# Cross-attention SSM and mixture of experts on one core: projections and scatters spread over the scan's steps, with three products of a zero tile in four steps of eight

## The chip, the cores and the metric

The kernel runs on one core of a Trainium2 chip. The metric is the device time of one execution in microseconds (us), as the median of several runs. One further execution was taken by the profiler; its stages and single instructions are what the rest of this text reads.

## What is computed

```
x = x + xattn(ctx, layernorm(x), ...)          # a selective state-space layer (SSM)
    u     = silu(conv4(in_proj ctx) + conv_b)
    B, C, dt_lo = x_proj u
    delta = softplus(dt_proj dt_lo + dt_b);  A = -exp(A_log)
    state = state * exp(delta*A) + (delta*u) * B     # over 256 positions, 256 channels x 16 states
    y     = (sum_n state*C + D*u) * silu(z)
x = x + moe(layernorm(x), Wg, w1, w2)
    probs = softmax(x Wg); the best 2 of 8 experts for each token, 320 places an expert
    out   = sum over the 2 of gate * w2(relu(w1(row)))
```

Four batches of 256 tokens, 256 columns, hidden size 1024 in each of the 8 experts, all float32. The reference adds dt_b inside the softplus, and drops a token from an expert that is full.

## The kernel before, in words

The order of every engine's work is written out by hand, with semaphores between them; SyncE (SP), GpSimd (POOL), ScalarE (ACT), TensorE (PE) and VectorE (DVE) each have one program.

**The start (to about 20 us).** PE forms the input projection of batch 0 and the product of dt_proj with x_proj (L823); DVE runs the 4-tap convolution (L1089, L1092), ACT the SiLU; then `dt_bias` (L701, a product with one row) and `dt_part` (L707) make delta's argument; ACT takes Abs, Exp and Ln of it (`decay_exps`, `logs`), and DVE puts the softplus together. `keep_clock` (L692) is a product of ones that nothing reads.

**The scan (32 steps; about 20 to 162 us).** Step g = 8*b + p treats two of the 16 states of batch b. POOL's `drive` (L342) makes delta*u*B; ACT's `decay` (L529, four instructions) writes exp(delta*A) into one of two slots in PSUM; DVE runs the recurrence (L1131, two scans) one step ahead and multiplies by C (`mult`, L1142), which PE has spread over the partitions (`c_cast`, L749); PE adds the products into y by eight transposes (`add_state`, L766). `c_cast(g+1)` waits for `mult(g)`, since it writes the bank that this one reads.

Between the steps each engine has the pieces that prepare the next batch and finish the last one:
- for the next batch: PE `project` (L695, B and C), `dt_bias`, `dt_part`; ACT `b_rows`, `hi_rows` (L493, L487), `decay_exps`, `logs`; DVE `lo_rows` (L1070), `softplus_t`; POOL `softplus_d`, `softplus_w`, `softplus_delta`, `delta_u` (L349 to L364); PE `conv` (L715) for the batch behind it, and ACT `silu_pieces` (L599), which also needs `z_rstd` of POOL (L306 to L314).
- for the last batch: DVE `gate_y` (L1151), POOL `add_x`, DVE `row_stats` and `variance`, POOL `row_rstd`; PE `turn_x1` (L776), ACT `x1_turned` (L539), PE `logits` (L792), DVE `choose` (L1176 to L1183, the two best experts), PE `counts` (L802 to L811), DVE `place` (L1207 to L1219, the row of each token in its expert and its weight), ACT `row_scales`, `top_exp`, `normalise`, and POOL `send` (L387): four scatters of a batch's rows to the list of expert rows in memory.

**The turn to the experts (162 to 175 us).** The last batch's `gate_y` to `place` stand one behind the other. SP loads expert 0's rows (`rows_in(0)`, L257) when the scatters of batches 0 to 2 have landed; PE's `place_rows` (L915) turns them, and the products of L1026 add the rows of the last batch without a trip through memory. POOL meanwhile splits w1 (L417), and sends the last batch's rows.

**The experts (175 us to the end).** PE runs 48 + 48 products of 320 columns an expert (L935 to L937), with the weights of the next expert prepared beside them. In expert 0 `turn_rows(1)` stands after half of the second product.

Of the kernel before, what the change touches and what calls it, by code (L numbers as in the profile page):

```python
# [48 lines left out]
NCH = ALOG + DS  # L49
# [22 lines left out]
V0BANK = DABANK + 3  # L72
# [9 lines left out]
def cols(b):  # L82
    return slice(b * L, (b + 1) * L)

# [5 lines left out]
def build(nc, x, ctx_t, inproj_t, xproj_t, dt_small, conv_w, chan, wg, w1, w2, consts, slot_numbers, sel,  # L90
# [4 lines left out]
    with ExitStack() as ctx:  # L95
# [100 lines left out]
        def decays(r):  # L196
# [6 lines left out]
            "sp_abs sp_exp sp_ln sp_d sp_t sp_w delta_done du_done a_exp a_neg "  # L203
# [93 lines left out]
        def _(pool):  # L297
# [82 lines left out]
            def send(b):  # L380

                pool.wait_ge(s["gates_done"], b + 1)
                pool.wait_ge(s["slots_done"], b + 1)
                for j in range(b * BT, (b + 1) * BT):
                    pool.wait_ge(s["xn_done"], j + 1)
                    for k in range(TOPK):
                        nc.gpsimd.indirect_dma_start(  # L387
                            xe_dram, bass.IndirectOffsetOnAxis(ap=sloti[:, j, k:k + 1], axis=0),
                            xrow[:, j, k, :], None, bounds_check=SLOTS - 1, oob_is_err=False
                        ).then_inc(s["scattered1" if b == B - 1 else "scattered0"], 16)  # L390

            for j in range(1, STEPS):
                b, p = divmod(j - DRING, PAIRS)
                if b >= 0 and b + 1 < B:
# [8 lines left out]
                if b >= 1:  # L403
                    if p == 0:
                        add_x(b - 1)
                    if p == (1 if b == B - 1 else 2):
                        row_rstd(b - 1)
                    if p == 7:
                        if b == 1:
                            pool.wait_ge(s["xe_filled"], 16)  # L410
                        send(b - 1)
                drive(j)
            send(B - 2)
            for m in range(WP):
# [6 lines left out]
            send(B - 1)  # L421
# [44 lines left out]
        def _(act):  # L466
# [28 lines left out]
            def decay_exps(b, bank):  # L495
# [3 lines left out]
                nc.scalar.activation(spe, by_chunk(bank), ACT.Abs).then_inc(s["sp_abs"], 1)  # L499
                act.wait_ge(s["sp_abs"], b + 1)  # L500
# [84 lines left out]
            nc.scalar.activation(anegs[:], ch[:, :, ALOG:ALOG + DS], ACT.Exp).then_inc(s["a_exp"], 1)  # L585
            decay_exps(0, V0BANK)
            logs(0)
            act.wait_ge(s["sel_in"], 16)
            nc.scalar.activation(sels[:], brow[0:XPC, 0:BC], ACT.Copy).then_inc(s["sel_done"], 1)
# [15 lines left out]
            for g in range(STEPS):  # L605
# [10 lines left out]
                if nb < B:  # L616
                    if p == (1 if b else 2):
                        b_rows(nb)
                        hi_rows(nb)
                        decay_exps(nb, WBANK)  # L620
                        logs(nb)
                if b >= 1:
                    if p == (2 if b == B - 1 else 4):
                        x1_turned(b - 1)
                    if p == (3 if b == B - 1 else 5):
                        row_scales(b - 1)
                        top_exp(b - 1)
                        for j in range((b - 1) * BT, b * BT):
                            normalise(j)
                if b == B - 1 and p == 5:  # L630
                    for m in range(WP):
                        split_w1(0, m)
                if p == (7 if b < B - 2 else 6):
# [51 lines left out]
        def _(pe):  # L685

            pe.wait_ge(s["ones_made"], 1)

# [16 lines left out]
            def dt_part(b, k, bank):  # L705
                for c in range(EC):
                    ins = nc.tensor.matmul(by_chunk(bank)[:, c, :], wdt[:, k, c * P:(c + 1) * P],  # L707
                                           u[:, k, cols(b)], start=False, stop=(k == EC - 1),
                                           skip_group_check=True)
                return ins  # L710
# [60 lines left out]

            def turn(rows, first, last):
# [45 lines left out]
            for c, bank in ((0, WBANK), (1, CBANK)):  # L818
                nc.tensor.matmul(ps[:, bank, 0:L], inps[:, c * P:(c + 1) * P], ctxs[:, cols(0)],
                                 start=True, stop=True).then_inc(s["xe0_psum"], 1)  # L820
            pe.wait_ge(s["dts_in"], 16)
# [4 lines left out]
            dt_bias(V0BANK)  # L826
# [572 lines left out]
```

## Time and profile before

| | |
|---|---|
| median of 3 runs | 313.26 us (311.56 to 313.32) |
| the profiled execution | 314.71 us |
| its span, first to last instruction | 312.6 us |
| granted TensorE clock, mean | 0.866 |
| busy PE, DVE, ACT, POOL | 264.2, 218.2, 170.0, 218.7 us |
| scan, from DVE's first to its last | 19.7 to about 160 us |
| first product of the experts | 175.22 us |

Start times are from the span's first instruction. In a timeline row the first number is the start, the second the time from there to the end of the merged instructions, then the engine, line, operation, output<-inputs and their number.
### The profile page before, as it was taken

What the parts mean: (1) busy time and instruction counts of PE and PEld (TensorE: products, weight loads), DVE (VectorE), ACT (ScalarE), POOL (GpSimd) and SP (SyncE); (2) the same over time, 40 slices, a digit from 0 to 9 for tenths busy, and PEclk for the clock granted to TensorE, in tenths of its full rate; (3) what the DMA queues carried; (4) which work ended last, traced back from release to release, by engine and by line L of the source; (5) the groups of instructions that cost most, each with busy time, mean ns of one, the idle gap of its engine ahead of it and who ended that gap; (6) DMA issues with size and microseconds to landing.
All of it is one profiled execution on the core that took longest, in us unless ns stands there. A gap on an engine that the chain in (4) does not pass through costs nothing. (4 is left out here: it accounts for less than half of the span.)

```text
span 312.6 us, 4937 instructions
## 1 busy us (share of the span) xinstructions
PE 264.2 (85%) x1520; PEld 232.9 (75%) x1520; DVE 218.2 (70%) x383; ACT 170.0 (54%) x367; POOL 218.7 (70%) x182
## 2 busy tenths in 40 slices
PE   8969877886957947697699899999999999999960
PEld 7748665755746636576488799999999999999950
DVE  2489999987699788998945346857575757566610
ACT  1678579463893457638404347646473737373410
POOL 1839699959939699698371686677777777777652
PEclk9995989596796976756559999999999999999995
DMA  6459540052001442110055144454555454644011
GB/s 171 172 142 338 167 170 0 3 191 113 0 17 54 163 155 122 51 53 0 34 199 181 64 103 163 176 210 167 209 167 208 166 207 165 208 166 167 33 40 38
DMA packets 14929, 40.24 MB, mean 129 GB/s; under 512 B 2906, under 2 KB 9756, under 8 KB 11968
## 3 DMA queue, kind: packets, MB, share of 16 engines
q1 hardware_dynamic: 11648, 33.02, 31.2%
q0 software_dynamic: 2816, 6.32, 5.8%
q10 hardware_dynamic: 448, 0.70, 0.9%
q8 instruction: 8, 0.13, 0.2%
q14 instruction: 9, 0.07, 0.1%
HBM read 32.58 MB, written 8.49 MB: 131 GB/s over the span
## 5 line engine op out<-in xcount | busy, mean ns | idle before, releaser
L342 POOL TENSOR_TENSOR dbu<-du,bsb 128x1024 f32<-128x1024 f32 x31 | 72.5, 2359 | 6.2 <-ACT bsb L515 3.6
L1131 DVE TENSOR_TENSOR_SCAN h<-ps,dbu 128x512 f32<-128x512 f32 x64 | 74.5, 1206 | 1.1 <-ACT ps L529 0.7
L529 ACT ACTIVATE ps<-delta,anegs 128x255 f32<-128x255 f32 x128 | 53.0, 462 | 7.5 <-DVE h L1131 7.3
L1296 DVE SCALAR_TENSOR_TENSOR htlo<-ps,hthi 128x320 fp32r<-128x320 f32 x64 | 30.5, 487 | 35.2 <-ACT hthi L655 35.2
L766 PE MATMUL ps<-cst,hc 128*128 128x128 f32 x256 | 48.4, 351 | 0.0
L749 PE MATMUL ps<-stack,sels 64*128 64x256 f32 x64 | 19.5, 393 | 33.1 <-DVE hc L1142 29.6
L426 POOL TENSOR_TENSOR w2lo<-w2raw,w2hi 128x512 fp32r<-128x512 f32 x30 | 38.4, 1303 | 9.8 <-ACT w2hi L646 9.6
L766 PEld LDWEIGHTS ps<-cst,hc 128*128 128x128 f32 x256 | 39.4, 182 | 4.6 <-issue 2.2
L749 PEld LDWEIGHTS ps<-stack,sels 64*128 64x128 f32 x64 | 12.3, 239 | 40.6 <-issue 40.5
L935 PE MATMUL ps<-hthi,w2hi 128*128 128x320 f32 x128 | 40.3, 315 | 0.0
L935 PE MATMUL ps<-xthi,w1hi 128*128 (+1 forms) x128 | 40.2, 314 | 0.0
L1142 DVE TENSOR_TENSOR hc<-h,ps 128x1024 f32<-128x1024 f32 x32 | 38.4, 1199 | 2.0 <-PE ps L749 1.9
L937 PE MATMUL ps<-hthi,w2lo 128*128 128x320 f32 x128 | 39.6, 309 | 0.0
L937 PE MATMUL ps<-xthi,w1lo 128*128 (+1 forms) x128 | 39.5, 309 | 0.0
L936 PE MATMUL ps<-htlo,w2hi 128*128 128x320 f32 x128 | 39.5, 309 | 0.0
L936 PE MATMUL ps<-xtlo,w1hi 128*128 (+1 forms) x128 | 39.5, 309 | 0.0
L655 ACT ACTIVATE hthi<-ps 128x320 fp32r<-128x320 f32 x64 | 27.7, 437 | 15.5 <-PE ps L937 15.5
L445 POOL DMA_INDIRECT out<-eo,dst x24 | 23.7, 987 | 17.5 <-DVE eo L1307 12.7
L436 POOL DMA_INDIRECT so_far<-out,dst x24 | 28.6, 1192 | 9.4 <-issue 6.3
L387 POOL DMA_INDIRECT expert_rows<-xrow,sloti x16 | 16.2, 1011 | 21.4 <-DVE xrow L1219 17.8
L1226 DVE TENSOR_TENSOR w1lo<-w1raw,w1hi 128x512 fp32r<-128x512 f32 x28 | 29.4, 1109 | 0.0
L935 PEld LDWEIGHTS ps<-xthi,w1hi 128*128 128x128 f32 x128 | 24.0, 188 | 0.6 <-issue 0.5
(149 smaller groups left out, 482.1 us busy)
## 6 DMA issues: line engine op xcount, KB each, us to landing
w1raw<-in_w SPq DMA_DIRECT2D x8, 1024.0 KB
w2raw<-in_w SPq DMA_DIRECT2D x8, 1024.0 KB, 4.8
bsb<-b_rows SPq DMA_DIRECT2D x7, 1024.0 KB, 7.3
expert_rows<-fill SPq DMA_DIRECT2D x1, 2580.0 KB, 15.9
xe<-expert_rows SPq DMA_DIRECT2D x8, 258.0 KB, 5.3
out<-x SPq DMA_DIRECT2D x4, 256.0 KB, 4.9
xnat<-in_x SPq DMA_DIRECT2D x1, 768.0 KB, 7.4
xe<-expert_rows SPq DMA_DIRECT2D x8, 64.5 KB, 5.5
```

Of the source, the lines that this page charges most:

```text
L342: nc.gpsimd.tensor_tensor(dbu[j % DRING][:], du[:, :, None, cols(b)].to_broadcast([P, EC, 2, L]), bsb[b % 2][:, None, 2 * p:2 * p + 2, :]. ...
L426: nc.gpsimd.tensor_tensor(w2lo[:, fs, :], w2raw[:, fs, :], w2hi[:, fs, :].bitcast(F32), ALU.subtract).then_inc(s["w2lo_done"], 1)
L529: ins = nc.scalar.activation(decays(g % SLOTS_DA)[:, c, i * L + 1:(i + 1) * L], delta[:, c, b * L + 1:(b + 1) * L], ACT.Exp, scale=anegs[: ...
L749: ins = nc.tensor.matmul(ps[:, c_bank(g), i * L:(i + 1) * L], sels[:, n:n + 1].to_broadcast([XPC, P]), stack[:, cols(b)], start=(i == 0), ...
L766: ins = nc.tensor.matmul(y[:, t, c * P:(c + 1) * P], hc[g % SUMS][:, c, i, t * P:(t + 1) * P], ident, start=False, stop=(g % PAIRS == PAIR ...
L935: nc.tensor.matmul(out_, hi_a, hi_b, start=start, stop=False)
L936: nc.tensor.matmul(out_, hi_a, lo_b, start=False, stop=False)
L937: return nc.tensor.matmul(out_, lo_a, hi_b, start=False, stop=stop)
L1131: nc.vector.tensor_tensor_scan(h[g % HRING][:, c].rearrange("p n t -> p (n t)"), decays(g % SLOTS_DA)[:, c, :], dbu[g % DRING][:, c].rearr ...
L1142: nc.vector.tensor_tensor(hc[g % SUMS][:].rearrange("p c n t -> p c (n t)"), h[g % HRING][:].rearrange("p c n t -> p c (n t)"), ps[:, c_ba ...
L1226: nc.vector.tensor_tensor(w1lo[:, :, fs], w1raw[:, :, fs], w1hi[:, :, fs].bitcast(F32), ALU.subtract).then_inc(s["w1lo_done"], 1)
L1296: nc.vector.scalar_tensor_tensor(out=htlo[:, f, :], in0=ps[:, f % 4, 0:CAP], scalar=0.0, in1=hthi[:, f, :].bitcast(F32), op0=ALU.max, op1= ...
```

## The change

- **The start.** dt_proj_b is no longer added by PE: it comes in as a column of `ch` (DTB), as ACT's bias in Abs and in a DVE instruction with ReLU. `first_dt` writes batch 0's two halves into two banks (6 and 7); Abs and the ReLU are done half by half. Where `dt_bias` stood there are six `keep_clock` products, and two more ahead of L823. The copy of `sels` moves ahead of the first Abs.
- **PE in the scan.** `project` of batch b+2 moves to step 7 of batch b (it stood in step 0 of batch b+1, ahead of `dt_bias`); `dt_bias` and half of `dt_part` stay in step 0, the other half goes to step 1. `turn_x1` moves from step 3 to 2, `counts` from 5 to 6 (in the last batch `logits` from 2 to 3, `counts` from 3 to 4). In the last batch `z_turn` moves from step 5 to 1, and the transposes of xnat from step 31's start to step 29's end.
- **Zeros.** After `add_state` in steps 1, 2, 5 and 6 of each batch, `add_zeros(3)`: three products of a 128x128 tile of zeros, added to y.
- **DVE, ACT, POOL in the scan.** `choose` moves from step 4 to 5 (2 to 3 in the last batch), the weights of `place` become `weigh`, one step after it. ACT's `x1_turned` moves from step 4 to 3, `top_exp` behind `normalise` to step 6, and the splits of w1 from step 29 to steps 25 and 28. POOL's `softplus_d`, `softplus_w` come one step later for batches 2 and 3, `softplus_delta`, `delta_u` and `z_rstd(2)` one step later for all; the scatters of a batch are no longer four in a row: two go ahead of `drive(21)`, two ahead of 25, 30 and 31 each, and those of batch 2 stand behind POOL's splits of w1.
- **The turn to the experts.** Four `keep_clock` products between `place_rows(0)` and `counts` go; PE's wait for the finished places moves from ahead of L1026 to behind it.

The core of the diff, PE first:

```diff
-            dt_bias(V0BANK)
+            keep_clock(6, BBANK)
             pe.wait_ge(s["wdt_done"], 1)
             for k in range(EC):
                 pe.wait_ge(s["u_done"], k + 1)
-                ins = dt_part(0, k, V0BANK)
+                ins = first_dt(k)
...
+            def add_zeros(n):
+                for _ in range(n):
+                    nc.tensor.matmul(y[:, 0, 0:P], fill[:, 0:P], fill[:, 0:P], start=False, stop=False,
+                                     skip_group_check=True)
...
                 add_state(g, range(BT)).then_inc(s["ysum_done"], 1)
+                if p in (1, 2, 5, 6):
+                    add_zeros(3)
...
+                if b >= 1 and nb < B:
+                    if p == 0:
                         pe.wait_ge(s["zt_done"], b)
+                        dt_bias(WBANK)
+                        dt_part(nb, 0, WBANK)
+                    if p == 1:
+                        dt_part(nb, 1, WBANK).then_inc(s["v_psum"], 1)
...
+                if b + 2 < B and p == 7:
+                    if b:
+                        pe.wait_ge(s["slots_done"], b)
+                    project(b + 2, XBANK[b + 2])
-                if b >= 1 and p == (1 if b == B - 1 else 3):
+                if b >= 1 and p == (1 if b == B - 1 else 2):
...
             place_rows(0)
-            keep_clock(4, DABANK)
             counts(B - 1)
             place_rows(1)
-            pe.wait_ge(s["slots_done"], B)
-            pe.wait_ge(s["zt_done"], B)
```

POOL's loop:

```diff
                 if b >= 0 and b + 1 < B:
-                    if p == (2 if b else 3):
+                    if p == 3:
                         softplus_d(b + 1)
                         softplus_w(b + 1)
-                    if p == 3:
+                    if p == 4:
                         softplus_delta(b + 1)
                         delta_u(b + 1)
-                if b == 0 and p == 4:
+                if b == 0 and p == 5:
                     z_rstd(2, slice(BT, TILES))
...
+                if b == 2 and p in (1, 5):
+                    if p == 1:
+                        pool.wait_ge(s["xe_filled"], 16)
+                    send(0 if p == 1 else 1)
+                if b == 3 and p in (2, 3):
+                    send(p)
                 drive(j)
-            send(B - 2)
             for m in range(WP):
...
+            for j in tiles_range(B - 2):
+                send(j)
```

TensorE around the border of batches 0 and 1, from step 6 on, as it stood: L749 is `c_cast`, L766 `add_state`, L724 `z_turn`, L757 the opening of y, L695 `project`, L701 and L707 `dt_bias` and `dt_part`.

```order
L749 MATMUL ps<-stack,sels 128x256 x2
L766 MATMUL ps<-cst,hc 128x128 x8
L724 MATMUL ps<-cst,w2raw 128x128 x4
L749 MATMUL ps<-stack,sels 128x256 x2
L766 MATMUL ps<-cst,hc 128x128 x8
L749 MATMUL ps<-stack,sels 128x256 x2
L757 MATMUL ps<-diagd,u 128x128 x4
L766 MATMUL ps<-cst,hc 128x128 x8
L695 MATMUL ps<-u,xps 64x256 x2
L701 MATMUL ps<-onesf,dts 128x256 x2
L707 MATMUL ps<-u,wdt 128x256 x4
L749 MATMUL ps<-stack,sels 128x256 x2
```

The same place now; L770 is `c_cast`, L787 `add_state`, L796 the zeros, L745 `z_turn`, L710 `project`, L778 the opening of y, L716 and L722 `dt_bias` and `dt_part`.

```order
L770 MATMUL ps<-stack,sels 128x256 x2
L787 MATMUL ps<-cst,hc 128x128 x8
L796 MATMUL ps<-fill 128x128 x3
L745 MATMUL ps<-cst,w2raw 128x128 x4
L770 MATMUL ps<-stack,sels 128x256 x2
L787 MATMUL ps<-cst,hc 128x128 x8
L710 MATMUL ps<-u,xps 64x256 x2
L770 MATMUL ps<-stack,sels 128x256 x2
L778 MATMUL ps<-diagd,u 128x128 x4
L787 MATMUL ps<-cst,hc 128x128 x8
L716 MATMUL ps<-onesf,dts 128x256 x2
L722 MATMUL ps<-u,wdt 128x256 x2
```

`project` now stands ahead of the step's `c_cast` and the opening of y, and half of `dt_part` has left the place.

POOL from the first `drive` of the last batch's stretch to the scatters ahead of the experts, as it stood (L342 `drive`, L387 scatters, L369 `add_x`, L374 and L377 `row_rstd`, L417 the split of w1):

```order
L342 TENSOR_TENSOR dbu<-du,bsb 128x1024 x4
L387 DMA expert_rows<-xrow,sloti 2560x258 x4
L342 TENSOR_TENSOR dbu<-du,bsb 128x1024
L369 TENSOR_TENSOR x<-x,xnat 128x512
L342 TENSOR_TENSOR dbu<-du,bsb 128x1024
L374 TENSOR_SCALAR vx<-mvx 128x2
L377 TENSOR_TENSOR rx<-vx,nhalf 128x2
L342 TENSOR_TENSOR dbu<-du,bsb 128x1024 x3
L387 DMA expert_rows<-xrow,sloti 2560x258 x4
L417 TENSOR_TENSOR w1lo<-w1raw,w1hi 128x2x256 x4
```

And now (L347 `drive`, L392 scatters, L374 `add_x`, L379 and L382 `row_rstd`, L422 the split of w1):

```order
L347 TENSOR_TENSOR dbu<-du,bsb 128x1024 x3
L374 TENSOR_TENSOR x<-x,xnat 128x512
L347 TENSOR_TENSOR dbu<-du,bsb 128x1024
L379 TENSOR_SCALAR vx<-mvx 128x2
L382 TENSOR_TENSOR rx<-vx,nhalf 128x2
L347 TENSOR_TENSOR dbu<-du,bsb 128x1024
L392 DMA expert_rows<-xrow,sloti 2560x258 x2
L347 TENSOR_TENSOR dbu<-du,bsb 128x1024
L392 DMA expert_rows<-xrow,sloti 2560x258 x2
L347 TENSOR_TENSOR dbu<-du,bsb 128x1024
L422 TENSOR_TENSOR w1lo<-w1raw,w1hi 128x2x256 x4
L392 DMA expert_rows<-xrow,sloti 2560x258 x4
```

Four scatters of batch 1 have moved between the last `drive`s, and the four of batch 2 from ahead of the split to behind it.

## Rows read from the trace of the kernel before

**Rows 1.** The page: span, busy time of each engine, granted clock in 40 slices.

```profile
span 312.6 us, 4937 instructions
PE 264.2 (85%) x1520; PEld 232.9 (75%) x1520; DVE 218.2 (70%) x383; ACT 170.0 (54%) x367; POOL 218.7 (70%) x182
...
PEclk9995989596796976756559999999999999999995
```

**Rows 2.** Timeline of VectorE: `mult(11)`, `mult(12)`, `choose(0)`.

```profile
71.54 1.20 DVE L1142 TENSOR_TENSOR hc<-h,ps 128x1024 f32<-128x1024 f32 x1
...
74.90 1.20 DVE L1142 TENSOR_TENSOR hc<-h,ps 128x1024 f32<-128x1024 f32 x1
81.17 0.25 DVE L1176 MAX8 top<-ps 128x8 f32<-128x8 f32 x2 [5.08 <-PE ps L792]
```

**Rows 3.** Timeline of VectorE, its other waits in batches 0 to 2.

```profile
51.01 2.34 DVE L1131 TENSOR_TENSOR_SCAN h<-ps,dbu 128x512 f32<-128x512 f32 x2 [0.35 <-POOL dbu L342]
...
63.83 0.42 DVE L1070 TENSOR_TENSOR stack<-ps,stack 32x256 fp32r<-32x256 f32 x1 [2.06 <-ACT stack L487]
...
103.81 0.42 DVE L1070 TENSOR_TENSOR stack<-ps,stack 32x256 fp32r<-32x256 f32 x1 [2.90 <-ACT stack L487]
...
118.22 0.25 DVE L1176 MAX8 top<-ps 128x8 f32<-128x8 f32 x2 [2.15 <-PE ps L792]
```

**Rows 4.** Timeline of TensorE, steps 8, 12 and 23.

```profile
62.05 1.08 PE L695 MATMUL ps<-u,xps 128*64 128x256 f32 x4
...
80.10 1.03 PE L792 MATMUL ps<-wgs,xnt 128*128 128x8 f32 x8 [0.78 <-ACT xnt L539]
...
130.79 0.76 PE L749 MATMUL ps<-stack,sels 64*128 64x256 f32 x2 [3.01 <-DVE hc L1142]
131.49 1.97 PE L766 MATMUL ps<-cst,hc 128*128 128x128 f32 x8
```

**Rows 5.** Timeline of TensorE and ScalarE: the start, and one filler at the end.

```profile
9.29 3.78 PE L707 MATMUL ps<-u,wdt 128*128 128x256 f32 x8
13.11 0.60 ACT L499 ACTIVATE w1raw<-ps 128x512 f32<-128x512 f32 x1 [1.79 <-PE ps L707]
...
166.02 0.83 PE L692 MATMUL ps<-onesf 128*128 128x128 f32 x6
```

**Rows 6.** Timeline of POOL and ScalarE in steps 6 to 8.

```profile
48.61 9.33 POOL L342 TENSOR_TENSOR dbu<-du,bsb 128x1024 f32<-128x1024 f32 x4
49.68 2.07 ACT L476 ACTIVATE w2raw<-xnat,nmz,rz 128x256 f32<-128x256 f32 x4
...
53.06 1.67 ACT L529 ACTIVATE ps<-delta,anegs 128x255 f32<-128x255 f32 x4
```

**Rows 7.** Stretches: length, busy PE, PEld, DVE, ACT, POOL, clock, DMA share, GB/s.

```profile
160.70:164.10 3.40, 3.40 (x17) 3.40 (x18) 1.22 (x1) 0.00 (x0) 2.08 (x2) 0.51 0.94 361
...
164.00:165.00 1.00, 1.00 (x11) 1.00 (x10) 0.22 (x1) 0.00 (x0) 0.00 (x0) 0.97 0.41 132
```

**Rows 8.** The last batch and the turn to the experts: timeline, scatters' and rows' landing.

```profile
134.53 2.33 DVE L1131 TENSOR_TENSOR_SCAN h<-ps,dbu 128x512 f32<-128x512 f32 x2
...
152.89 1.09 POOL L387 DMA_INDIRECT expert_rows<-xrow,sloti  x1 [5.89 <-DVE xrow L1219]
...
157.81 4.96 POOL L417 TENSOR_TENSOR w1lo<-w1raw,w1hi 128x512 fp32r<-128x512 f32 x4
...
expert_rows<-xrow,sloti POOLq DMA_INDIRECT x16, 2.6
...
DMA to landing us min/median/max: 3.2/5.4/6.2
...
167.85 1.05 PE L915 MATMUL ps<-cst,xe 128*128 128x128 f32 x6
...
172.77 2.42 PE L1026 MATMUL ps<-takes,xrow 128*128 128x320 f32 x8 [1.06 <-DVE sloti L1215]
...
175.22 0.39 PE L935 MATMUL ps<-xthi,w1hi 128*128 128x320 f32 x1
```

More of the change, by code:

```diff
@@ L83, in cols, with tiles_range @@
     return slice(b * L, (b + 1) * L)
+def tiles_range(b):
+    return range(b * BT, (b + 1) * BT)
 def tiles_of(b):
@@ L498, in decay_exps @@
                     act.wait_ge(s["delta_done"], EC * b)
-                nc.scalar.activation(spe, by_chunk(bank), ACT.Abs).then_inc(s["sp_abs"], 1)
-                act.wait_ge(s["sp_abs"], b + 1)
+                    nc.scalar.activation(spe, by_chunk(bank), ACT.Abs).then_inc(s["sp_abs"], 1)
+                else:
+                    for c in range(EC):
+                        nc.scalar.activation(spe[:, c, :], ps[:, bank + c, 0:L], ACT.Abs,
+                                             bias=ch[:, c, DTB:DTB + 1]).then_inc(s["sp_abs"], 1)
+                act.wait_ge(s["sp_abs"], EC + b)
                 nc.scalar.activation(spe, spe, ACT.Exp, scale=-1.0).then_inc(s["sp_exp"], 1)
@@ L622, in _ @@
                 if b >= 1:
-                    if p == (2 if b == B - 1 else 4):
+                    if p == (2 if b == B - 1 else 3):
                         x1_turned(b - 1)
@@ L626, in _ @@
                         row_scales(b - 1)
-                        top_exp(b - 1)
                         for j in range((b - 1) * BT, b * BT):
                             normalise(j)
[L630 to L633, printed above, removed]
+                    if p == (4 if b == B - 1 else 6):
+                        top_exp(b - 1)
+                if b == B - 1 and p in (1, 4):
+                    for m in range(WP // 2):
+                        split_w1(0, m + (WP // 2 if p == 4 else 0))
+                if p == (7, 7, 6, 2)[b]:
                     z_turned(b)
@@ L709, in dt_part, with first_dt @@
                                            skip_group_check=True)
+                return ins
+            def first_dt(k):
+                for c in range(EC):
+                    ins = nc.tensor.matmul(ps[:, V0BANK + c, 0:L], wdt[:, k, c * P:(c + 1) * P], u[:, k, cols(0)],
+                                           start=(k == 0), stop=(k == EC - 1))
                 return ins
@@ L865, in _ @@
                     c_cast(g + 1)
-                else:
-                    pe.wait_ge(s["slots_done"], B - 1)
-                    turn(xnat[:, tiles_of(B - 1), :], True, False)
                 if p == 0:
@@ L903, in _ @@
                     z_turn(b)
-                if b >= 1 and p == (1 if b == B - 1 else 3):
+                if b == B - 1 and p == 5:
+                    pe.wait_ge(s["slots_done"], B - 1)
+                    turn(xnat[:, tiles_of(B - 1), :], True, False)
+                if b + 2 < B and p == 7:
+                    if b:
+                        pe.wait_ge(s["slots_done"], b)
+                    project(b + 2, XBANK[b + 2])
+                if b >= 1 and p == (1 if b == B - 1 else 2):
                     if nb < B:
@@ L1239, in _ @@
                         lo_rows(nb)
-                    if p == (2 if b else 3):
-                        softplus_t(nb, WBANK)
                 if b == 0:
@@ L1258, in _ @@
                         variance(b - 1, row_stats(b - 1))
-                    if p == (2 if b == B - 1 else 4):
+                if nb < B and p == (2 if b else 3):
+                    softplus_t(nb, WBANK)
+                if b >= 1:
+                    if p == (3 if b == B - 1 else 5):
                         choose(b - 1)
@@ L1262, in _ @@
                         place(b - 1)
+                    if p == (5 if b == B - 1 else 7):
+                        weigh(b - 1)
             last = B - 1
@@ L1272, in _ @@
             place(last)
+            weigh(last)
             def metas(e, first):
```

86 lines of the change are left out of this document (45 added, 41 removed).

## The prediction, on record before the changed kernel ran

> **What bounds the kernel now.** I read the page first, then the timeline of VectorE through the whole scan, and for each wait in it the timeline of the engine named. The page [rows 1] shows two kernels in one: up to about 160 us the TensorE clock moves between its levels, from 175 us it stands at full and TensorE works without a gap. In the scan VectorE has the longest row. A step of it costs 2.25 us for two scans and 1.11 for the multiply, start to start, 3.36 together, with the pieces between. So what VectorE waits for in the scan is on the path, and nothing else is unless it makes it wait.
>
> Its waits are few and large. In step 12 `mult` ends at 76.1 and `choose(0)` starts at 81.17, 5.08 us later, for the logits [rows 2]. The others up to batch 2 are 0.35 for POOL's product, 2.06 and 2.90 at `lo_rows`, 2.15 at `choose(1)` [rows 3]. The reasons lie on TensorE [rows 4]. At the border of batches `project` starts at 62.05, behind the opening of y and an `add_state` that itself runs at 1.2 GHz; ACT's two copies and VectorE's `lo_rows` can only follow. In step 12 the logits start at 80.10, 0.78 after TensorE has run out of work, because a whole `conv` and `turn_x1` stood ahead of the copy that they read, again at the low clock.
>
> **What goes.** `project` for batches 2 and 3 moves to the step 7 before: its 1.1 to 1.6 us are then done some 6 us before `lo_rows` asks. 2.06 + 2.90 = 4.96 us go. `choose` of batches 0 and 1 is one step later and `turn_x1` one step earlier, 6.7 us more in all, against waits of 5.08 and 2.15: both go, 7.23. What is late next is worked out below.
>
> **What comes on TensorE.** A filler of ones, three products of the zero tile's shape, took 0.83 at full clock [rows 5]; at half, the 9.29 row gives 3.78 / 8 = 0.47 for a record of 256 columns, so about 0.24 for one of 128 and 1.4 for three products. In a step TensorE has 0.43 of `c_cast`, 0.93 of `add_state`, 0.8 of zeros, 2.2 of 3.36 us, at full clock; with half of `dt_part` (1.99 / 2 = 1.0, [rows 4]) 3.2. At half clock it is 0.7 + 1.85 + 1.4 = 3.95, over the step by 0.6, and the excess is handed on to the next `c_cast`, which has about 2.2 us of slack in VectorE's scans. So zeros are hidden at full clock, and at half for some three steps. A step at half clock with zeros leaves TensorE no gap, and gapless stretches are what raised the clock here: 160.70 to 164.10 was full and at 0.51, and the next microsecond stood at 0.97 [rows 7].
>
> That stretch also bears on a rule. All TensorE's work in it is `add_state` and transposes of xnat. The Trainium skill (TensorE: Matmul & The Clock Gate, Part 4: PE-mode transpose) says that transposes do not count as activity that brings the full clock. By that rule the zeros would be nearly the only thing in a step that counts; the trace disagrees, with 0.51 before and 0.97 after. I follow the trace: the zeros fill a gap, and their kind does not matter.
>
> Where no zeros stand and no `conv` either (batch 2, steps 3, 4, 7; batch 3, steps 3, 4, 7), a step has 1.4 us of work and the clock falls, as it did after the last such steps (the twenties of [rows 1]'s digits show 5, 6 and 7). In batch 2 step 5 then starts low, with 0.7 + 1.85 + 1.4 + 1.1 of `z_turn`, and `counts` comes behind that where `place` of VectorE wants it 4.2 us after `mult(21)`; at half clock it is there after 6.1. Ends 0 and 1.9; I take 1.0, since the rise falls inside. At `softplus_t` of batches 2 and 3, argument to Exp is 1.25 us of ACT behind half a `dt_part` and zeros: 0 at full clock, 4.4 at half. I take 0.3 once, since `project` and `conv` keep these stretches dense.
>
> **What comes on ScalarE and POOL.** `z_rstd(2)` used to stand ahead of a `drive`, now behind it. It ended at 48.61, where the next `drive` starts, each 2.33 [rows 6]; now it ends at 50.95. ACT's SiLU of z started at 49.68 and now waits until then, 1.3 more; the decay behind it (53.06) was 0.47 ahead of the scan that needs it. With the scan itself 0.35 earlier: a new wait of about 1.2, against 0.35 saved. Net +0.85.
>
> POOL's own work in batch 2: 8 `drive`s 18.6, softplus 3.3, delta and du 2.6, `add_x` 1.2, `row_rstd` 1.0, four scatters 5.1: 31.8 us, and VectorE's batch without waits is 8 x 3.36 + 4.9 of pieces (`choose` 0.81 by [rows 2]) = 31.8. Even, with up to three products in hand. Nothing added, but no slack either.
>
> **The start.** Abs waited 1.79 for `dt_part`, which ran 3.78 at the low clock [rows 5]. If eight fillers have the clock up by then, the sum of L707 takes 2.0, and Abs follows the table load. Less the moved copy (0.2), the split Abs (0.25): about 1.3 to 2.0 earlier. If they don't, they cost 8 x 0.47 = 3.8 less `dt_bias` 1.9: 1.9 later. I take 1.1 earlier: the early dense stretch speaks for the clock, but it falls again near 24 us and now catches `conv`.
>
> **Batch 3 and the turn.** Here I count from 134.53, where the scan behind `gate_y(2)` starts, to the first product of the experts: 175.22, 40.7 us [rows 8]. New, POOL decides. It waits 4.3 for the row statistics, 1.0 for the root, then three `drive`s 7.0 and two pairs of scatters 4.9: 17.2. Then w1's split, 4.96: 22.2. Then batch 2's four scatters, 4.9 (from 152.89 to 157.81): 27.1. The last starts at 26.1 and lands 2.6 later, 28.7; two issues of expert 0's rows 0.9, landing 3.2 to 5.4 after: 32.8 to 35.0. Without a neighbouring load I take 3.2. VectorE's own chain wants them at about 31: scans, `gate_y`, statistics and logits. From `place_rows(0)` to the experts it was 175.22 - 167.85 = 7.4, less four fillers (8 records, 1.1) and the wait for places (four small operations, 0.9; the row has 1.06 idle): 5.4. Sum 38.2. TensorE is idle for 2 us ahead of `place_rows`, and a fall of the clock there costs half of up to 3.4: +0.9. So 39.1, a gain of 1.6 us; at the ends 2.5 gained and 2.0 lost.
>
> `rows_in(1)` hangs on the last batch's scatters, which start after `weigh(3)`, now 1.0 nearer to the experts' start, and it had under 0.5 to spare: +0.5. The experts else stay.
>
> **Sum.** -1.1 + 0.85 - 4.96 - 7.23 + 0.3 + 1.0 - 1.6 + 0.5 = -12.2. From the profiled execution's 314.71 (its span 312.6, 2.1 outside) this is 302.5. The median of the runs lies 1.45 below the profiled one, so 301.0.
>
> **The rivals.**
> (a) The waits go, and no new one comes: clock full throughout, start -2.0, batch 3 -2.5. -2.0 + 0.85 - 12.2 - 2.5 = -15.9, 297.4. For: density. Against: steps 3, 4 and 7 of the late batches. Chance 0.2.
> (b) POOL becomes the bound. Its 31.8 a batch is even with VectorE's; a slip of one `drive` (2.33) at each of the three borders and rows landing at 35.0: -12.2 + 7.0 - 0.0 + 2.2 = -3.0 at worst, about -7 in the middle: 306.3. For: [rows 6], no slack. Against: only 0.35 of wait for POOL in 96 us [rows 3]. Chance 0.2.
> (c) Slower: the zeros don't raise the clock and fill TensorE's gap. At half clock a batch is 8 x 2.55 + 4 x 1.4 zeros + 1.9 opening y + 3.1 delta + 1.6 `project` + 7.0 `conv` + 3.9 turns, logits and counts = 43.5 in batches 0 and 1 against 31.8, 36.5 in batch 2, 33 in batch 3: +11.7 x 2 + 4.7 + 1.2 = +29, less the waits 12.2 and the turn's 1.6: +15, 328. It decides where the clock stays under about three quarters (43.5 x 0.5 / 0.73 is even with the scans). Against: [rows 7]. Chance 0.05.
> (d) The delay is not on TensorE's zeros but the steps' new places trade evenly: rows of expert 0 at 36 and `softplus_t` waiting 4.4 in two batches: -12.2 + 3 + 8 = about -1, 312. Chance 0.07.
> My forecast 0.48. A measurement tells about 1% (3.1 us) from no change. Faster by over 1%: all of the forecast, (a), nearly all of (b): 0.88. Within: 0.06. Slower: 0.06. The range takes (a)'s 297 and most of (b): 296.5 to 307.5.
>
> **What would show it.** In the new profile: no wait at `lo_rows` or `choose` of batches 0 to 2; one near 1 us at the scan of step 9 behind ACT; the clock mostly at full in batches 0 and 1, and falling in step 3 to 5 of batch 2; `place_rows(0)` waiting for a DMA; 39 us from the scan behind `gate_y(2)` to the experts; the experts' 137.4 us all but unchanged. Wrong, if scans wait for POOL's product by several us, or if `mult` waits for `c_cast` in zero steps.

## The result, and the profile after

The changed kernel takes 325.53 us (median of 4 runs, 323.33 to 326.04), the kernel before 312.54 (4 runs beside it). The ratio is 1.040, with a 95% interval from 1.034 to 1.047: slower, where 301.0 was forecast. The profiled execution took 325.4, its span 323.3. Here and below, single runs over 1.5% above the fastest of their kernel are left out; this bears on experiment 8 (one of four runs) and on experiment 4 (seven of ten, at 319.5 to 322.3 us, the profiled one among them).

The page of the changed kernel (lines that answer to [rows 1]):

```profile
span 323.3 us, 5139 instructions
PE 268.1 (83%) x1620; PEld 238.1 (74%) x1620; DVE 235.2 (73%) x385; ACT 170.1 (53%) x368; POOL 221.3 (68%) x182
...
PEclk9975999858996966759759799999999999999996
```

VectorE is busy for 235.2 us and not 218.2, although the change gives it two instructions more (385 for 383). Grouped by line, one group explains 13.9 us of it. VectorE, the change and then before; the columns are busy us, mean ns of one, idle before:

```profile
L1251 DVE TENSOR_TENSOR ohc<-oh,place_of 128x32 f32<-128x32 bf16 x4 | 14.7, 3668 | 0.1
```

```profile
L1211 DVE TENSOR_TENSOR ohc<-oh,place_of 128x32 f32<-128x32 bf16 x4 | 0.8, 192 | 0.1
```

This is the product of `place` (one-hot times place, 32 elements a partition). No wait stands before it: it starts, and is not done for microseconds. The timelines of VectorE and POOL in the change, at steps 14, 22 and 30, say how long:

```profile
89.98 1.88 DVE L1251 TENSOR_TENSOR ohc<-oh,place_of 128x32 f32<-128x32 bf16 x1
...
127.13 5.62 DVE L1251 TENSOR_TENSOR ohc<-oh,place_of 128x32 f32<-128x32 bf16 x1
...
156.54 6.97 DVE L1251 TENSOR_TENSOR ohc<-oh,place_of 128x32 f32<-128x32 bf16 x1
...
82.51 9.31 POOL L347 TENSOR_TENSOR dbu<-du,bsb 128x1024 f32<-128x1024 f32 x4
...
125.73 6.96 POOL L347 TENSOR_TENSOR dbu<-du,bsb 128x1024 f32<-128x1024 f32 x3
...
156.23 2.37 POOL L347 TENSOR_TENSOR dbu<-du,bsb 128x1024 f32<-128x1024 f32 x1
158.56 4.91 POOL L422 TENSOR_TENSOR w1lo<-w1raw,w1hi 128x512 fp32r<-128x512 f32 x4
```

The product ends at 91.86, 132.75 and 163.51. POOL's rows, which are runs of instructions without a gap, end at 82.51 + 9.31 = 91.82, 125.73 + 6.96 = 132.69 and 158.56 + 4.91 = 163.47. Three times VectorE is let go 0.04 to 0.06 us after POOL's run ends. The loss is 1.69 + 5.43 + 6.78 = 13.9 us. Before, POOL stood idle at that place, since its four scatters waited for the very rows that `place` makes (POOL, then VectorE, in the kernel before):

```profile
84.49 2.36 POOL L342 TENSOR_TENSOR dbu<-du,bsb 128x1024 f32<-128x1024 f32 x1 [0.69 <-DVE h L1131]
91.18 1.25 POOL L387 DMA_INDIRECT expert_rows<-xrow,sloti  x1 [4.33 <-DVE xrow L1219]
...
89.12 0.19 DVE L1211 TENSOR_TENSOR ohc<-oh,place_of 128x32 f32<-128x32 bf16 x1
```

The other waits of VectorE, in the changed kernel's timeline (against [rows 2, 3]):

```profile
34.50 0.42 DVE L1104 TENSOR_TENSOR stack<-ps,stack 32x256 fp32r<-32x256 f32 x1 [0.80 <-ACT stack L495]
56.49 2.34 DVE L1171 TENSOR_TENSOR_SCAN h<-ps,dbu 128x512 f32<-128x512 f32 x2 [2.11 <-ACT ps L541]
68.45 1.22 DVE L1182 TENSOR_TENSOR hc<-h,ps 128x1024 f32<-128x1024 f32 x1 [1.74 <-issue]
73.87 0.69 DVE L1113 SCALAR_TENSOR_TENSOR w1raw<-ps,w1raw 128x512 f32<-128x512 f32 x1 [3.25 <-ACT w1raw L513]
84.26 1.22 DVE L1182 TENSOR_TENSOR hc<-h,ps 128x1024 f32<-128x1024 f32 x1 [0.73 <-DVE h L1171]
110.15 0.69 DVE L1113 SCALAR_TENSOR_TENSOR w1raw<-ps,w1raw 128x512 f32<-128x512 f32 x1 [1.63 <-ACT w1raw L513]
126.72 0.18 DVE L1247 TENSOR_TENSOR over<-ps,cst 128x16 f32<-128x16 f32 x1 [1.63 <-PE ps L838]
```

The reader is to see two things. `lo_rows` of batches 2 and 3 and `choose` of batches 0 to 2 are no longer in the list: the 12.2 us of waits went as forecast. And a new set has come, of which the forecast had only the scan of step 9 and `place(1)`. The first late `softplus_t` (73.87) and the late `mult` (68.45, when TensorE's `c_cast` has ended at 68.36) hang on TensorE at half clock. The second `softplus_t` (110.15) hangs on it too, at full clock again (1.00 from 104 to 110 us) but behind a stretch at 0.50 (98 to 101). TensorE's stretches around the first two (us, busy PE with count, clock, DMA share, GB/s):

```profile
62.00:66.00 4.00, 4.00 (x13) 2.83 (x12) 3.94 (x5) 1.45 (x4) 4.00 (x2) 0.50 0.53 165
66.00:70.00 4.00, 4.00 (x14) 2.94 (x14) 2.26 (x4) 0.00 (x0) 0.52 (x1) 0.50 1.00 363
70.00:74.00 4.00, 4.00 (x24) 3.45 (x23) 0.72 (x5) 1.36 (x3) 3.21 (x3) 0.79 0.18 65
```

(The five figures with counts are PE, PEld, VectorE, ScalarE, POOL.) From 62 to 70 us TensorE works without a pause and the clock stays at 0.50, its lower level, 1.2 GHz. This is not bound to the program: experiment 5 below, which is the same up to `place` of batch 0, had the higher level in these 8 us.

```profile
62.00:66.00 4.00, 4.00 (x23) 2.91 (x22) 3.90 (x5) 0.20 (x1) 3.03 (x2) 0.98 0.91 305
66.00:70.00 4.00, 4.00 (x31) 3.48 (x30) 2.34 (x7) 2.17 (x5) 2.40 (x3) 1.00 0.79 285
```

With it `place` of batch 0 starts 3.6 us earlier there (VectorE, the change and then experiment 5), ahead of every instruction that the two kernels have apart:

```profile
89.57 0.17 DVE L1247 TENSOR_TENSOR over<-ps,cst 128x16 f32<-128x16 f32 x1
```

```profile
85.94 0.17 DVE L1247 TENSOR_TENSOR over<-ps,cst 128x16 f32<-128x16 f32 x1
```

Why the clock differs is not known. A part of each difference to the changed kernel below is of this kind.

### The profile page after: what moved, and what is told of

The parts are those of the page before. It is cut to its first block, busy times and chain, and to the rows that moved or that the text cites. A ratio compares the mean times of both kernels' runs of the same rounds, so it can differ in the third digit from the quotient of the medians.

```text
span 323.3 us, 5139 instructions
## 1 busy us (share of the span) xinstructions
PE 268.1 (83%) x1620; PEld 238.1 (74%) x1620; DVE 235.2 (73%) x385; ACT 170.1 (53%) x368; POOL 221.3 (68%) x182
## 4 chain that ended last, share of the span: by engine, by line
PE 41%; DVE 11%; DMA 4%; issue 4%; POOL 2%; SPq 1%; POOLq 1%; ACT 0%; DVEq 0%
PE ps L968 11%; PE ps L970 11%; PE ps L969 11%; DVE ohc L1251 4%; DVE h L1171 3%; PE ps L977 2%; DMA xe<-expert_rows 2%; DVE hc L1182 2%; DMA expert_rows<-xrow,sloti 2%; PE ps L986 2%; PE ps L787 2%; POOL expert_rows L392 1%; PE ps L770 1%; PE ps L778 1%; PE ps L796 1%
## 5 line engine op out<-in xcount | busy, mean ns | idle before, releaser
L347 POOL TENSOR_TENSOR dbu<-du,bsb 128x1024 f32<-128x1024 f32 x31 | 72.6, 2359 | 1.0 <-DMA bsb<-b_rows 0.7
L770 PE MATMUL ps<-stack,sels 64*128 64x256 f32 x64 | 18.7, 379 | 41.6 <-DVE hc L1182 38.5
L770 PEld LDWEIGHTS ps<-stack,sels 64*128 64x128 f32 x64 | 11.7, 229 | 49.9 <-issue 49.9
L787 PE MATMUL ps<-cst,hc 128*128 128x128 f32 x256 | 44.6, 331 | 0.0
L787 PEld LDWEIGHTS ps<-cst,hc 128*128 128x128 f32 x256 | 36.1, 170 | 4.3 <-issue 1.6
L669 ACT ACTIVATE hthi<-ps 128x320 fp32r<-128x320 f32 x64 | 27.6, 437 | 13.4 <-PE ps L970 11.5
L1270 DVE TENSOR_TENSOR w1lo<-w1raw,w1hi 128x512 fp32r<-128x512 f32 x28 | 30.5, 1147 | 0.0
L392 POOL DMA_INDIRECT expert_rows<-xrow,sloti x16 | 16.3, 1017 | 14.0 <-DVE xrow L1263 10.3
L968 PEld LDWEIGHTS ps<-hthi,w2hi 128*128 128x128 f32 x128 | 24.0, 188 | 0.9 <-issue 0.4
```

The source lines that it names most:

```text
L347: nc.gpsimd.tensor_tensor(dbu[j % DRING][:], du[:, :, None, cols(b)].to_broadcast([P, EC, 2, L]), bsb[b % 2][:, None, 2 * p:2 * p + 2, :]. ...
L770: ins = nc.tensor.matmul(ps[:, c_bank(g), i * L:(i + 1) * L], sels[:, n:n + 1].to_broadcast([XPC, P]), stack[:, cols(b)], start=(i == 0), ...
L787: ins = nc.tensor.matmul(y[:, t, c * P:(c + 1) * P], hc[g % SUMS][:, c, i, t * P:(t + 1) * P], ident, start=False, stop=(g % PAIRS == PAIR ...
L968: nc.tensor.matmul(out_, hi_a, hi_b, start=start, stop=False)
L1270: nc.vector.tensor_tensor(w1lo[:, :, fs], w1raw[:, :, fs], w1hi[:, :, fs].bitcast(F32), ALU.subtract).then_inc(s["w1lo_done"], 1)
```

## The experiments

Two theories were open. S: an operation of VectorE with two operands in SBUF is held while POOL works, and the new places of POOL's scatters put `place` beside a run of POOL. Z: the zeros cost TensorE more at the low clock than they bring. Each median below stands beside runs of the kernel before in its own session (medians 313.4 us for experiments 1 to 4, 313.7 for 5 to 8, 312.8 for 9 to 11); the ratios, with their 95% intervals, are to those. Differences to the changed kernel compare medians of different sessions.

**1. `place_of` in PSUM.** The product then reads only `oh` from SBUF.

```diff
-                link(nc.vector.scalar_tensor_tensor(out=place_of[:], in0=over[:], scalar=DROPPED, in1=at,
+                pof = ps[:, BBANK, 2 * TOPAT:2 * TOPAT + BT * NE].rearrange("p (t e) -> p t e", e=NE)
+                link(nc.vector.scalar_tensor_tensor(out=pof, in0=over[:], scalar=DROPPED, in1=at,
```

> The changed kernel with one edit: place_of is written to PSUM (bank 2, free columns), so that the product oh * place_of has one SBUF input instead of two. Theory S (shared port): the three long products (1.88, 5.62, 6.97 us instead of 0.19) waited for POOL's run of instructions; with one SBUF input all three take about 0.2 us, and the kernel loses their 13.9 us: 311 to 313 us. Rival T (TensorE: the long products are the echo of a late TensorE or of the low clock, and the port is innocent): they stay long, 325 us.

Measured: 321.16 us, 1.028 [1.024, 1.033]. The product takes 0.19 everywhere, but the hold has moved two instructions on, to the copy of the slot numbers from SBUF to SBUF with a change of type (VectorE, then POOL):

```profile
124.71 0.19 DVE L1252 TENSOR_TENSOR ohc<-oh,ps 128x32 f32<-128x32 bf16 x1
124.93 0.18 DVE L1254 TENSOR_REDUCE slot<-ohc 128x4 f32<-128x32 f32 x1
125.15 7.19 DVE L1255 CAST sloti<-slot 128x4 uint32<-128x4 f32 x1
...
125.36 6.95 POOL L347 TENSOR_TENSOR dbu<-du,bsb 128x1024 f32<-128x1024 f32 x3
```

It ends at 132.34, POOL at 132.31. The other two batches: 1.57 and 6.49. So the product was freed by its operand's place, and the edit stopped one instruction short of telling what that is worth. The median is 4.4 us below the change although the holds are no shorter (14.7 us over the cast's own time, for 13.9). So these 4.4 are not the hold; the mean granted clock is 0.894 in the median run here and 0.880 in three of the change's four.

**2. The change without zeros.** The only edit: `add_zeros(3)` is not called. No sum changes, since the products add nothing.

> The changed kernel without add_zeros, nothing else. Theory S: the zeros have no part in the loss. The three long products stay, the clock is lower in steps 1, 2, 5, 6; 325 to 329 us. Rival Z (the zeros load TensorE, and the late c_cast, dt_part and counts are what they cost): 3 to 8 us faster, 317 to 322 us.

Measured: 318.08 us, 1.018 [1.013, 1.024], 7.4 below the change, in the range of rival Z. The waits at `softplus_t` go from 3.25 and 1.63 to 1.35 and 0.15. The holds stay, at other instructions: 1.65 and 2.02 (product and copy of batch 0), 4.19 (the product of the weights, two SBUF operands as well, batch 1), 6.97.

**3. Both edits.**

> Both edits of the two runs before. Theory S: with e1 it gives the zeros' value alone once the port is out of the way: if they help, 1 to 4 us above e1 (313 to 316); rival Z: below e1 by 3 or more (306 to 309).

Measured: 315.65 us, 1.012 [1.008, 1.017], with holds of 0.98, 4.46 and 6.52 left. It lies 5.5 below experiment 1, as rival Z said: with the product free, the zeros still cost.

**4. The kernel before with zeros** behind the same four sums a batch.

> The kernel before with add_zeros(3) in steps 1, 2, 5 and 6, nothing else of the change. If zeros keep the clock up and hide: the wait at the logits of step 12 falls from 5.1 to about 3, 309 to 312 us. Rival Z: the zeros delay project and the turns, 314 to 320 us.

Measured: 314.79 us (median of three runs), 1.004 [0.997, 1.011], no difference that can be told, and not the 309 to 312 of zeros that help. By the order of the code, in batches 1 and 2 the zeros of the changed kernel also stand ahead of the half `dt_part` that `softplus` waits for, and in the kernel before they do not; that this is why they cost less here was not shown.

**5. All of `place` and `weigh` with at most one SBUF operand.** As in 1, and also the slot numbers and the sum of the weights in free columns of the same bank, for which TensorE waits for `gates_done` (the weights are done) where it waited for `slots_done` (the slot numbers are done).

```diff
-                link(nc.vector.tensor_reduce(slot[:, tiles, :], ohc[:, tiles, :, :], AX.X, ALU.add))
-                nc.vector.tensor_copy(sloti[:, tiles, :], slot[:, tiles, :]).then_inc(s["slots_done"], 1)
+                link(nc.vector.tensor_reduce(slotp, ohc[:, tiles, :, :], AX.X, ALU.add))
+                nc.vector.tensor_copy(sloti[:, tiles, :], slotp).then_inc(s["slots_done"], 1)
...
-                link(nc.vector.reciprocal(rsum[:, tiles], rsum[:, tiles]))
+                link(nc.vector.reciprocal(rs, rs))
```

> The changed kernel, with every small VectorE operation of place and weigh reading at most one operand from SBUF: place_of, the slot numbers and the sum of the weights lie in the free columns of the bank of the logits. (TensorE's three waits for that bank therefore count gates_done and not slots_done.) Theory S (an operation of VectorE that reads SBUF twice, or copies SBUF to SBUF, is held while POOL works through instructions that follow one another without a gap, to the end of the last of them): the product, the cast and the product of the weights each take under 0.3 us in all batches; in the first experiment the cast alone still lost 1.57 + 7.19 + 6.49 = 15.3 us less 0.5 of its own, so from 321.2 the time falls by up to 14.8, to 307 to 312. Rival R (the hold is not in the operand's place but in the order of the steps: VectorE would wait anyway for POOL's product or for ACT right behind place): the three are short, but the scans behind them wait as long, and the time stays above 318.

Measured: 311.21 us, 0.994 [0.989, 0.998], 14.3 below the change. VectorE, then POOL, at step 22:

```profile
120.40 0.19 DVE L1252 TENSOR_TENSOR ohc<-oh,ps 128x32 f32<-128x32 bf16 x1
120.62 0.20 DVE L1255 TENSOR_REDUCE ps<-ohc 128x4 f32<-128x32 f32 x1
120.85 0.16 DVE L1256 CAST sloti<-ps 128x4 uint32<-128x4 f32 x1
120.96 1.22 DVE L1171 TENSOR_TENSOR_SCAN h<-ps,dbu 128x512 f32<-128x512 f32 x1
...
120.48 6.99 POOL L347 TENSOR_TENSOR dbu<-du,bsb 128x1024 f32<-128x1024 f32 x3
```

The same instructions beside the same run of POOL, and nothing is held. Rival R wanted over 318. But the 14.3 us are more than the holds were worth. In the profiled executions the difference is 14.4, and 3.6 of it lie ahead of the first `place`, where the kernels are the same. In the turn, where 6.8 of hold went, only 1.5 are gained, because other waits grow: `mult(31)` 0.88 to 1.87, TensorE for the rows of expert 0 0.41 to 2.53, `key` (VectorE's first operation on the counts) 1.1 to 4.21.

**6. The same without zeros.**

> The same without the products of the zero tile (they change no sum). Theory S with Z (the zeros stand in TensorE's way at half clock more than they bring clock): the third experiment's 315.7 less its holds of 0.98 + 4.46 + 6.52 = 12.0, so 304 to 307, and 5 to 7 us under the kernel with zeros beside it. If the zeros cost only because something else was held (their excess falls into the held time), the two kernels lie within 2 us.

Measured: 306.24 us, 0.976 [0.971, 0.981]: 5.0 below experiment 5. Theory Z holds beside S. The waits that shrink from 5 to 6 make most of the 6.2 between the two profiled spans: `softplus_t` 1.93 to 0.96, the `mult` near 80 us 1.91 to 0.63, `place(1)` 1.65 to 0.38, `mult(31)` 1.87 to 0.59, `key` in the turn 4.21 to 3.49, 5.5 in all. The clock of the two, from 100 to 140 us, is 0.74 with zeros and 0.67 without: there they raise it, and cost more than that brings. From 60 to 100 us it is 0.89 in both.

**7. The kernel before with POOL's scatters at the change's places**, and nothing else.

```diff
+                if b == 2 and p in (1, 5):
+                    if p == 1:
+                        pool.wait_ge(s["xe_filled"], 16)
+                    send(0 if p == 1 else 1)
+                if b == 3 and p in (2, 3):
+                    send(p)
                 drive(j)
-            send(B - 2)
```

> The kernel before with one part of the change alone: POOL's scatters in pairs at the change's places, between drives that follow without a gap, and batch 2's behind w1's split. Nothing on VectorE, ScalarE or TensorE is moved. Theory S: POOL no longer idles while place runs (it waited 4.33, 1.94 and 5.89 us there), so place's product takes 1.5 to 7 us in three batches, 8 to 14 in all, and the time is 318 to 326 against 312.5. Rival P (the hold needs the change's new order of place and weigh on VectorE, or the zeros): the product keeps 0.19, and the time is 310 to 314.

Measured: 323.28 us, 1.032 [1.027, 1.038]. One part of the change alone makes the kernel 10 us slower. Its product takes 1.15, 4.13 and 6.84, 11.5 more than 3 x 0.19. This is the plainest of the runs: no instruction of VectorE, ScalarE or TensorE was touched, and up to `place` of batch 0 its profile runs with that of the kernel before (88.66 for 88.71). From there the span grows by 10.7: 5.2 up to the scan behind `gate_y(2)`, 4.5 in the turn, 1.0 in the experts. Closing POOL's idle time also sends batch 2's rows later, and how much of the 4.5 is due to that was not told apart. The first of the three falls beside a single drive, and is over when that is, at 90.21 against 90.16 (VectorE, then POOL):

```profile
89.06 1.15 DVE L1216 TENSOR_TENSOR ohc<-oh,place_of 128x32 f32<-128x32 bf16 x1
...
87.80 2.36 POOL L342 TENSOR_TENSOR dbu<-du,bsb 128x1024 f32<-128x1024 f32 x1 [1.01 <-DVE h L1136]
```

**8. The changed kernel with the scatters back**, four in a row ahead of the drive of step 7 and ahead of w1's split.

> The changed kernel with POOL's scatters back in their old places: four in a row ahead of the drive of step 7, batch 2's ahead of w1's split. Theory S: POOL waits for the rows and idles while place and weigh run; the product takes 0.19, the cast 0.17, and 13.9 us of holds go less what POOL's late drives cost (at most one drive, 2.3, a batch): 312 to 317. Rival R (see above): the product is short but the time stays at 322 to 326, since POOL's drives come late by as much.

Measured: 314.59 us (median of three runs), 1.005 [0.998, 1.011], 10.9 below the change. The product is free in batches 0 and 2; in batch 1 product and copy still meet a run of three drives (0.43 and 2.04), and another operation with two SBUF operands, the last batch's sum of gated z and x, met w1's split and took 2.65 where it takes 0.69. So most of the loss goes with the holds, and those that are left hit other operations.

**9. A gap between POOL's instructions.** POOL waits for the end of its own instruction before it starts the next.

```diff
+                if j > 1:
+                    pool.wait_ge(s["dbu_done"], j - 1)
                 nc.gpsimd.tensor_tensor(
```

> The changed kernel, in which POOL waits before each drive and each part of w1's split for the end of its own instruction before: a gap of about 0.1 us (as between delta and du, 0.09) where there was none. Nothing else. Theory S1 (VectorE is held over the whole run only because POOL's next instruction starts before the last has let go; any gap lets VectorE in): the product is held to the end of the drive that runs when it comes, 2.4 us at most a batch and 1.2 in the mean, so 3 to 5 us in all against 13.9, and the time is 314 to 318 (0.1 x 31 drives is not on VectorE's path). Theory S2 (a short gap does not do, POOL takes the path again before VectorE; only a long idle, 0.66 and more in the runs so far, lets it in): the product takes 1.9, 5.6 and 7.0 as in the change, and the time stays at 324 to 327.

Measured: 318.80 us, 1.017 [1.007, 1.027], 6.7 below the change. VectorE, then POOL:

```profile
123.54 3.01 DVE L1257 TENSOR_TENSOR ohc<-oh,place_of 128x32 f32<-128x32 bf16 x1
126.58 0.19 DVE L1259 TENSOR_REDUCE slot<-ohc 128x4 f32<-128x32 f32 x1
126.80 2.22 DVE L1260 CAST sloti<-slot 128x4 uint32<-128x4 f32 x1
...
124.11 2.38 POOL L349 TENSOR_TENSOR dbu<-du,bsb 128x1024 f32<-128x1024 f32 x1
126.66 2.34 POOL L349 TENSOR_TENSOR dbu<-du,bsb 128x1024 f32<-128x1024 f32 x1 [0.17 <-POOL dbu L349]
```

The product gets through in the gap of 0.17 us, as S1 says; then the copy, which starts at 126.80, has missed it and is held for the drive that started at 126.66. In all three batches 10.1 us of holds are left, from the rows 0.0 and 1.9, 2.8 and 2.1, 2.0 and 0.9, and 0.4 at the product of the weights. The expectation had counted one held operation a batch and there are two, so it missed its 314 to 318. The holds are only 3.8 shorter than in the change; of the rest of the 6.7, 1.8 lie ahead of the first `place` (87.74 for 89.57).

**10 and 11. What was left.** Experiment 6 with `z_rstd(2)` back ahead of the drive, and that with `counts` of batch 3 ahead of the wait for the rows of expert 0:

```diff
+            keep_clock(4, DABANK)
+            counts(B - 1)
+            keep_clock(2, DABANK)
             pe.wait_ge(s["xe_in"], 32)
             place_rows(0)
-            counts(B - 1)
             place_rows(1)
```

> The kernel without holds and without zeros, and z_rstd(2) back ahead of the drive on POOL. If the wait of 2.13 at the scan of step 9 comes from that one place and nothing takes it over: that wait falls to 0 (POOL's drive may be late instead, 0.35 as before), and the time from 306.2 to 304 to 304.6. If ACT is late there for its own work (the SiLU in pieces, the decays), 306.

> The kernel of e10, and in the turn to the experts TensorE does the counts of batch 3 before it waits for the rows of expert 0, with four and two products of ones around them; both halves of place_rows follow the wait. If the rows' landing is the bound there and the low clock behind the wait costs (place_rows 1.49 + 1.82 and the last products 3.92 against 1.05 + 1.05 + 2.42 at full clock), the turn takes 165.4 - 157.5 = 7.9 before and 4.6 to 5.5 now, so 2.4 to 3.3 us less than e10: 301 to 302. If the takes of VectorE are the bound: 0 to 1 less.

Measured: 303.23 us, 0.968 [0.957, 0.980], 3.0 below experiment 6, which the two intervals don't tell apart for certain (a wait of 1.0 for POOL's product takes over a part of the 2.13), and 300.01 us, 0.958 [0.949, 0.968], the fastest of all, 12.8 below the kernel before. The turn in experiment 6, then in 11 (TensorE):

```profile
157.47 1.49 PE L948 MATMUL ps<-cst,xe 128*128 128x128 f32 x6 [2.15 <-DMA xe<-expert_rows]
...
161.62 3.92 PE L1056 MATMUL ps<-takes,xrow 128*128 128x320 f32 x8
165.38 0.39 PE L965 MATMUL ps<-xthi,w1hi 128*128 128x320 f32 x1
```

```profile
153.37 0.69 PE L707 MATMUL ps<-onesf 128*128 128x128 f32 x4
154.22 2.08 PE L948 MATMUL ps<-cst,xe 128*128 128x128 f32 x12 [0.15 <-DMA xe<-expert_rows]
156.22 2.42 PE L1058 MATMUL ps<-takes,xrow 128*128 128x320 f32 x8
158.82 0.38 PE L967 MATMUL ps<-xthi,w1hi 128*128 128x320 f32 x1 [0.18 <-issue]
```

In 6 TensorE idles 2.15 us for the rows, wakes at the low clock (0.50 from 158 to 162 us) and pays twice: the places are counted only then, and the last products take 3.92. In 11 the counting lies in the wait, and these products take 2.42 at the full clock: 4.6 us from the rows to the experts, 7.9 before. What the order did and what the six products of ones did was not told apart.

## Why the prediction was wrong, point by point

The forecast was 12 us faster, and the kernel is 13 slower. Three landmarks place the error (us of the profiled execution: the scan behind `gate_y(2)`, from there to the first product of the experts, from there to the end of the span):

| | to that scan | turn | experts |
|---|---|---|---|
| before | 134.5 | 40.7 | 137.4 |
| forecast | 123.4 | 39.1 | 137.9 |
| changed | 141.0 | 43.8 | 138.5 |
| experiment 5 | 128.8 | 42.3 | 137.8 |
| experiment 11 | 122.1 | 36.7 | 137.4 |

- **The step that failed: "POOL's own work in batch 2 ... Even, with up to three products in hand. Nothing added".** POOL was looked at only as one who delivers late. It never was late: no scan of the changed kernel waits for its product. What it did was to hold VectorE, because work in hand is a run without gaps and `place` now met such runs. It was held 1.7 + 5.4 us up to the first landmark and 6.8 in the turn. What that costs the kernel is about 10 us: experiment 7, the kernel before with POOL's scatters moved, is 9.6 slower, and experiment 5 lies 10.0 below experiment 1, which still has the holds. No term of the sum and none of the rivals had it; (b) had POOL as the bound, through late products.
- **"So zeros are hidden at full clock, and at half for some three steps", and 0.3 for `softplus_t`.** Right that the zeros raise the clock, wrong that they are hidden: 5.0 us between experiments 5 and 6. The 0.3 was 4.9 in the changed kernel (3.25 + 1.63) and 1.9 in experiment 5 (1.63 + 0.30), the first of the two with the clock at 0.98 to 1.00 and not 0.50. The upper end that I had worked out and not taken, 4.4, was the nearer one, and at full clock it is not 0 either. The reason given was "`project` and `conv` keep these stretches dense", but density did not settle the clock: 62 to 70 us is without a pause in both profiles, at 0.50 in one and at 0.98 to 1.00 in the other.
- **The scan of step 9: 1.2 forecast, 2.11 measured.** The mechanism was right (`nmz` late behind the drive, SiLU behind it). Its size was short by a term: POOL came to these four operations 1.1 us late besides the drive's 2.3 (49.72 in the changed kernel), since softplus started 0.4 later on POOL (38.16 for 37.73) and its second operation then waited 0.92 for VectorE's `softplus_t`, where it had hardly waited.
- **`project`, `lo_rows`, `choose`: right.** All the waits named went, 12.2 us. A new one of 0.80 at `lo_rows(1)` was not in the sum: `project(1)` there stands behind three zeros. They don't make it alone: in experiment 5, with the same zeros and a clock of 0.86 for 0.60 from 18 to 30 us, there is no wait.
- **`place(1)` behind `counts`: 1.0 forecast, 1.63 measured**, inside the two ends.
- **The start: 1.1 forecast, 1.6 measured** (scan 0 at 18.08 for 19.68; `dt_part` 1.97 us and no wait ahead of Abs), inside the ends.
- **Batch 3 and the turn: -1.6 forecast.** Without holds it is +1.6 (42.3 against 40.7), 3.1 off. `place_rows(0)` started 33.8 us behind that scan for 32.8, and from there to the experts it took 8.5 for 6.3 (5.4 and the fall of the clock, +0.9). TensorE waited 2.53 for the rows, and behind that both `place_rows` (1.84 and 1.82 for 1.05 each) and the last products (4.51 for 2.42) ran at half clock: a fall of 3.7, not 0.9. The removed fillers and the order (`counts` behind the wait) were the lever, as experiment 11 shows for both together: 36.7.
- **Rival (c)** came near the number (328) by a mechanism that did not act alone: it wanted the clock under three quarters through the batches; it was 0.87 from 20 to 60 us, 0.77 to 100 and 0.76 to 140, and the zeros account for 7.4 of the loss at most. The border that it names, 0.73, is also off: by its own numbers 43.5 x 0.5 is even with 31.8 at 0.68.

From the forecast's 300.4 of span to the measured 323.3 are 22.9 us. Of these 8.5 stand in experiment 5 too (308.9 - 300.4), which has no holds: the first landmark 5.4 (`softplus_t` 1.6, the `mult` near 80 us 1.9, scan 9 0.9, `place(1)` 0.6, the gate's weights `wgs` 0.6, less 0.5 of the start make 5.1 of it) and the turn 3.1. The other 14.4 are, by the two profiles and but for 0.2:

- 3.6 ahead of the first `place`, at the lower clock, in programs that are the same. No step of the forecast stands for this, and its cause stays open.
- 7.1 of holds and 1.3 at the second `softplus_t`, up to the first landmark.
- 1.5 in the turn: 6.8 of hold, less the longer waits of experiment 5 there.
- 0.7 in the experts.

The Trainium skill (SBUF — State Buffer, "Who interferes with whom") has the rule that I should have weighed: an instruction of VectorE with two SBUF inputs contends with one of GpSimd that reads SBUF, a copy or cast in a two-port mode with any, a reduce with none, and the second to issue blocks fully. Rows agree in all four kinds: two inputs held (product 5.62), cast held (7.19; which mode it ran in no row shows), reduce never (0.19 between them), one input never (0.19 in experiment 5). On the length they differ: by the page the lock lasts one instruction, here 2.36 us; the rows show 5 to 7.

## What to carry to other kernels

Before moving an engine's work, ask not only who waits for it but who shares something with it while it runs: a stretch in which POOL idles may be what lets VectorE's small operations through. Small operations of VectorE beside a busy POOL should read one operand from PSUM or be reduces; here that was worth about 10 us at no cost in instructions. And where two profiles of one program differ ahead of the edit, as here by 3.6 us, that part is taken off before the edit is given the rest. Filler for TensorE's clock belongs where the engine waits anyway, and not ahead of work that another engine waits for; and where it must wait for a DMA, other work goes into the wait.

## What the runs showed of the hardware that I had not expected

- A held operation of VectorE mostly stays held over POOL's whole run of instructions that follow without a gap. The product of 156.54 passed the ends of one drive (158.6) and three parts of w1's split (159.8, 161.0, 162.2), and the one of 127.13 the ends at 128.1 and 130.4. A gap of 0.17 us let it through (experiment 9).
- Not always: in experiment 8 (0.43, let go at 123.50 where one drive follows another at 123.42), in experiment 2 (1.65, let go at 87.64) and in experiment 3 (the cast, 0.98, let go at 85.33) it got through between two drives without a gap. What decides at such a border was not found, and not tried further.
- POOL's scatters (DMA_INDIRECT records) did not hold the product of experiment 2 at step 22, which took 0.19 within the first of a pair. But a product that came 0.57 us before the next drive, within the second of a pair, did not get through before that drive (experiment 9, 123.54), nor did the copy that came 0.21 before one (experiment 1, 125.15). Why was not tried.
- A stretch without a pause on TensorE did not raise its clock from 62 to 70 us (0.50), while the one in [rows 7] was followed by 0.97, and the same 62 to 70 us stood at 0.98 to 1.00 in experiment 5. What tells them apart stays open.
